# Weight sums by VectorE, later edge preparation, and a residual that is added from its two parts

## The reference

```python
xn = layernorm(x)                                            # 1250 x 1024
# graph part, 40000 edges (src, dst, type), 8 relations
u = xn @ root + bias
for r in range(8):                                           # mean of the neighbours of type r
    sums = segment_sum(xn[src] * (edge_type == r), dst)
    u = u + (sums / max(count_r, 1)) @ weight[r]
z = concat([u, xn]) @ w_gate + b_gate
gnn = tanh(u) * z + xn * (1 - z)
# linear attention, 16 heads of 64
q, k = elu(xn @ Wq) + 1, elu(xn @ Wk) + 1
v, g = xn @ Wv, sigmoid(xn @ Wg + bg)
mix = ((q * scale) @ (k^T v)) / clip(q . sum(k)) * g @ Wo
x1 = x + gnn + mix
# gated cell; the state starts at 0, so the forget gate falls out
y = layernorm(x1)
i, o, c = sigmoid(y @ Wi + bi), sigmoid(y @ Wo2 + bo), tanh(y @ Wc + bc)
out = x1 + o * tanh(i * c)
```

## Time and profile before

| what | us |
|---|---|
| median of the timed runs | 2199.6 |
| lowest and highest | 2197.4, 2200.03 |
| the profiled execution | 2188.48 |
| its span | 2186.7 |
| busy in it: TensorE, weight loads, VectorE, ScalarE, POOL | 2118.5, 1708.9, 1297.6, 538.6, 808.0 |

### The profile page before, as it was taken

How to read it: one execution, slowest core, us unless ns; L and a number is a source line. 1 busy time by engine, 2 the same in 40 slices (tenths; PEclk the granted TensorE clock), 3 DMA queues, 4 the chain that set the end, 5 groups by cost and what they waited for, 6 DMA issues and landing times.

```text
span 2186.7 us, 25371 instructions
## 1 busy us (share of the span) xinstructions
PE 2118.5 (97%) x9562; PEld 1708.9 (78%) x9562; DVE 1297.6 (59%) x1705; ACT 538.6 (25%) x749; POOL 808.0 (37%) x663
## 2 busy tenths in 40 slices
PE   7979897989999999999999999999999999999999
PEld 6767675768888888888877778888988887888887
DVE  5555778665666666666656666773354658534233
ACT  4433353501111111100121211012232313321121
POOL 3248134025555556543646445541211353000000
PEclk9999898999999999999999999999999999999999
DMA  7986675778588888883987878974159998604102
GB/s 273 344 282 196 220 248 173 250 206 303 173 288 309 314 295 308 280 288 116 317 281 270 279 260 296 306 229 163 61 172 263 282 294 270 175 23 126 56 34 80
DMA packets 248145, 497.68 MB, mean 228 GB/s; under 512 B 39442, under 2 KB 71873, under 8 KB 248023
## 3 DMA queue, kind: packets, MB, share of 16 engines
q1 hardware_dynamic: 165782, 279.20, 39.1%
q0 software_dynamic: 65248, 191.13, 26.2%
q10 hardware_dynamic: 16992, 25.73, 3.6%
HBM read 403.60 MB, written 133.45 MB: 246 GB/s over the span
## 4 chain that ended last, share of the span: by engine, by line
PE 90%; DVE 4%; DMA 2%; issue 1%; POOL 1%; SPq 1%; ACT 0%; POOLq 0%; ACTq 0%; DVEq 0%
PE acc L1412 71%; PE acc L1383 12%; PE acc L1407 5%; POOL runs L2375 1%; PE acc L1320 1%; DMA Wraw<-in_L_gnn_weight 1%; DVE Wlo L1708 1%; PE misc L1305 1%; DMA sample_d<-samples 1%; DMA made<-y_d 1%; SPq L861 0%; DVE below L1834 0%; PE tp L1267 0%; DMA runs<-code_d,run_row 0%; PE acc L1420 0%
## 5 line engine op out<-in xcount | busy, mean ns | idle before, releaser
L1412 PE MATMUL acc<-Whi,aThi 128*128 128x512 f32 (+1 forms) x2232 | 882.0, 395 | 0.0
L1412 PE MATMUL acc<-Whi,aTlo 128*128 128x512 f32 (+1 forms) x2232 | 879.1, 394 | 0.0
L1412 PE MATMUL acc<-Wlo,aThi 128*128 128x512 f32 (+1 forms) x2232 | 876.5, 393 | 0.0
L2395 POOL DMA_INDIRECT ring<-y_d,edge x390 | 484.1, 1241 | 425.7 <-DVE U L1984 144.1
L1412 PEld LDWEIGHTS acc<-Whi,aTlo 128*128 128x128 f32 (+1 forms) x2232 | 413.7, 185 | 103.5
L1412 PEld LDWEIGHTS acc<-Wlo,aThi 128*128 128x128 f32 (+1 forms) x2232 | 414.4, 186 | 102.4
L1412 PEld LDWEIGHTS acc<-Whi,aThi 128*128 128x128 f32 (+1 forms) x2232 | 413.6, 185 | 102.0 <-DVE made L1756 0.3
L1708 DVE TENSOR_TENSOR Wlo<-Wraw,Whi 128x1024 fp32r<-128x1024 f32 x176 | 224.0, 1275 | 161.1 <-ACT Whi L1438 160.2
L1383 PE MATMUL acc<-Whi,aThi 128*128 128x512 f32 (+2 forms) x560 | 229.4, 410 | 54.1 <-DVE Wlo L1708 33.1
L1984 DVE SCALAR_TENSOR_TENSOR U<-ring,edge,U 128x1024 f32<-128x1024 f32 x180 | 230.3, 1280 | 31.6 <-DMA ring<-y_d,edge 31.3
L1984 DVE SCALAR_TENSOR_TENSOR odd<-ring,edge,odd 128x1024 f32<-128x1024 f32 x170 | 217.7, 1280 | 36.4 <-DMA ring<-y_d,edge 35.9
(11 more groups left out here) (209 smaller groups left out, 1566.5 us busy)
## 6 DMA issues: line engine op xcount, KB each, us to landing
Wraw<-in_L_gnn_weight SPq DMA_DIRECT2D x80, 512.0 KB, 8.0
y_d<-res SPq DMA_DIRECT2D x80, 256.0 KB, 2.3
...
```

Of the source, the lines that this page charges most:

```text
L1412: mm = nc.tensor.matmul(to, a[:, k, rows(i)], b[:, s % 2, k, :], start=start, stop=stop)
L2395: pool.indirect_dma_start(ring[:, j % RING, :], None, a, bass.IndirectOffsetOnAxis(ap=index, axis=0), bounds_check=top - 1, oob_is_err=Fal ...
```

## The change

There are five parts.

1. The 32 weight sums are VectorE's, one per slot (q, k): for BE_ at units 3, 4 and 5 of the stage before, steps 1 and 5; for GA_0 at (39, 5) and (40, 5), for the others twenty units later each.
2. POOL no longer adds x + xnb, and xs_d is gone with its ten stores. The buffer of an x tile is free for the next load when the tile is normalised and turned.
3. In the output stage SP loads x into bias_sb and xn_d into the res buffer (`load_normal`, behind the wait that the store of unit q-3 has landed), and VectorE adds the two ahead of its wait for the product, then adds the product.
4. At the start SP issues five weight pieces before x1 instead of four, then three, then x2 and x3; the raw edges are loaded in unit 8.
5. The edge preparation is two units later, and tables_weights is cut into four pieces: (97, 7), (98, 2), (98, 6), (99, 2) and (126, 3), (126, 7), (127, 3), (127, 7).

```diff
-SUM_BESIDE = {BE_: (2, 2, 3, 3, 4, 5), GA_: (-1, 0)}
+SUM_BESIDE = {BE_: ((3, 1), (3, 5), (4, 1), (4, 5), (5, 1), (5, 5)), GA_: ((-1, 5), (0, 5))}
-READS_AT = 43
+READS_AT = 45
 def edge_at(q, k):
     if q < 36:
-        return divmod(212 + (8 * (q - 17) + k) * 21 // 16, 8)
-    return divmod(424 + (8 * (q - 36) + k) * 61 // 32, 8)
+        return divmod(228 + (8 * (q - 17) + k) * 21 // 16, 8)
+    return divmod(440 + (8 * (q - 36) + k) * 61 // 32, 8)
...
         # SP, at the start
         load_x(0)
-        for n in SPLIT_ORDER[0:4]:
+        for n in SPLIT_ORDER[0:5]:
             load_w(n)
         load_x(1)
-        load_w(SPLIT_ORDER[4])
-        load_w(SPLIT_ORDER[5])
+        for n in SPLIT_ORDER[5:8]:
+            load_w(n)
         load_x(2)
-        load_w(SPLIT_ORDER[6])
-        load_w(SPLIT_ORDER[7])
         load_x(3)
...
         def x_rows(t):
             sp.wait_ge(ln_done, with_halves(t))
             sp.dma_start(xn_d[side(t), :], xnb[0:SIDES[t % 5], t % XS, :]).then_inc(xn_st[t % XS], 16)
-            sp.wait_ge(xs_made, t + 1)
-            sp.dma_start(xs_d[side(t), :], xr[0:SIDES[t % 5], t % XS, :]).then_inc(xs_st[t % XS], 16)
         def next_x(t):
-            sp.wait_ge(xs_st[t % XS], 16 * (t // XS + 1))
+            sp.wait_ge(ln_done, with_halves(t))
             load_x(t + XS)
...
         # SP, output stage
-        sp.dma_start(bias_sb[0:width(t), t % 2, :], xs_d[rows(t), half(h)]).then_inc(xs_in[t % 2], 16)
+        sp.dma_start(bias_sb[0:width(t), t % 2, :], x[rows(t), half(h)]).then_inc(xs_in[t % 2], 16)
+        def load_normal(q):
+            s, t = UNIT[q]
+            free_res(sp, q)
+            sp.dma_start(res[0:width(t), q % 3, :], xn_d[rows(t), half(STAGE[s][2])]).then_inc(xs_in[t % 2], 16)
...
         # VectorE, evict(q)
+        if kind == O_:
+            dve.wait_ge(xs_in[i % 2], XS_FROM + 32 * (T // 2 * h + i // 2 + 1))
+            chain(nc.vector.tensor_tensor(bias_sb[0:w, i % 2, :], bias_sb[0:w, i % 2, :], res[0:w, q % 3, :],
+                                          ALU.add))
+            dve.wait_ge(prod, q + 1)
+            nc.vector.tensor_tensor(res[0:w, q % 3, :], p, bias_sb[0:w, i % 2, :], ALU.add).then_inc(evac_v, 1)
+            return
...
         # VectorE's list; add_quarters is POOL's of before, with nc.vector and dve
+        if (q, k) in SUMS_AT:
+            add_quarters(*SUMS_AT[q, k])
...
-        if (q, k) == edge_at(59 + 15 * h, 1):
-            tables_weights(h)
+        for piece in range(4):
+            if (q, k) == edge_at(58 + 15 * h, 4 + 2 * piece):
+                tables_weights(h, piece)
...
         # POOL
-        def rows_sum(t):
-            pool.wait_ge(ln_done, with_halves(t))
-            a = xr[0:SIDES[t % 5], t % XS, :]
-            nc.gpsimd.tensor_tensor(a, a, xnb[0:SIDES[t % 5], t % XS, :], ALU.add).then_inc(xs_made, 1)
```

More of the change, by code:

```diff
@@ L242 @@
 for _s in range(BLOCK_STAGES):
[L243 to L244 removed]
+    for (_g, _n), (_o, _k) in zip(SUM_ORDER.get(STAGE[_s][0], ()), SUM_BESIDE.get(STAGE[_s][0], ())):
+        SUMS_AT[FIRST[_s - 1] + _o, _k] = (_s, _g, _n)
 def sums_to(s, g, n):
@@ L434, in build @@
         x1n_d = dram("x1n_d", [N, D])
-        xs_d = dram("xs_d", [N, D])
         ax_d = dram("ax_d", [128, K, N])
@@ L601, in build @@
         xn_st = [sem(f"xn_st{i}") for i in range(XS)]
-        xs_st = [sem(f"xs_st{i}") for i in range(XS)]
-        ln_var, ln_root, ln_done, xs_made, x_turned, x_hi, x_lo = (
-            sem(n) for n in ("ln_var", "ln_root", "ln_done", "xs_made", "x_turned", "x_hi", "x_lo"))
+        ln_var, ln_root, ln_done, x_turned, x_hi, x_lo = (
+            sem(n) for n in ("ln_var", "ln_root", "ln_done", "x_turned", "x_hi", "x_lo"))
         t4_st = x1n_st = [sem(f"t4_st_x1n_st{i}") for i in range(2)]
@@ L1744, in lo_left, with add_quarters, add @@
                                         ALU.subtract).then_inc(a_lo, 1)
+            def add_quarters(s, g, n):
+                def add(to, of):
+                    nc.vector.tensor_tensor(to, to, of, ALU.add).then_inc(w_sum, 1)
+                kind, at = STAGE[s][0], GRAN * s + g
+                if kind == BE_ and n > 1:
+                    dve.wait_ge(w_sum, sums_to(s, g, n - 1))
+                    add(granule(Wraw, at) if n == 2 else granule(Whraw, at + 2), granule(Wraw, at + 2 if n == 2 else at))
+                    return
+                dve.wait_ge(w_raw[at % (2 * GRAN)], raw_to(at, 2))
+                if kind == BE_:
+                    dve.wait_ge(w_raw[(at + 2) % (2 * GRAN)], raw_to(at + 2, 2))
+                    add(granule(Wraw, at + 2), granule(Whraw, at))
+                else:
+                    add(granule(Wraw, at), granule(Whraw, at))
             def evict_middle(q):
@@ L2103, in evict @@
                 dve.wait_ge(prod, q + 1)
-                if kind == O_:
-                    n = T * h + i
-                    dve.wait_ge(xs_in[i % 2], XS_FROM + 16 * (T // 2 * h + i // 2 + 1))
-                    nc.vector.tensor_tensor(res[0:w, q % 3, :], p, bias_sb[0:w, i % 2, :], ALU.add).then_inc(evac_v, 1)
-                    return
                 n = BIASED.index(s)
@@ L2447, in _ @@
             pool.wait_ge(w_lo, 2 * GRAN)
-            rows_sum(0)
             for t in range(T):
@@ L2466, in _ @@
                            allow_small_or_imprecise_dtypes=True).then_inc(place_const, 1)
-            rows_sum(1)
-            for t in range(2, T):
-                rows_sum(t)
             for q in range(BLOCK_UNITS):
-                for s, g, n in SUMS_AT.get(q, ()):
-                    add_quarters(s, g, n)
                 reads = q - READS_AT
```

90 lines of the change are left out of this document (41 added, 49 removed).

## The result

The changed kernel takes 2174.43 us by the median of four timed runs (three lie between 2170.37 and 2174.65; the fourth took 4235.76, about twice as long, of unknown cause, and is left out of the ratio) against 2199.43 for four of before, a ratio of 0.988 (95% interval 0.986 to 0.990). The forecast was 2171, with a range from 2154 to 2188. Its profiled execution took 2174.2 us, with a span of 2172.4. The gain on the median is 25.0 us; between the two profiled executions it is only 14.3. Between the first two profiles the forecast's total hides two errors of 11 and 13 us that met; a second pair of profiles, further down, leaves less of both.

A forecast was written before the change was run, and what follows sets the result against it. TensorE was taken as the bound, busy 2118.5 of 2186.7 us, leaving at most 68.2 us idle to win. Terms summed to 28.0 us, giving 2160.5 profiled and, with 11.1 carried over, 2171; range 2154 to 2188.

The forecast's parts named there:

- start-up order: At the start, a weight piece before x1 shortens TensorE's 3.99 us stop: 1.9 us gained, between 0 and 2.5.
- rows_sum and xs_d, to unit 21: Without POOL's row sums and stores, tile 8 of x comes in time: 3.5 us gained, between 1 and 4.
- units 36 to 41: Block stage: Whraw lands earlier and six sums run faster on VectorE: 9.3 us gained, between 4 and 14.
- units 41 to 62: Block stage: uninterrupted reads and unstretched operations cut VectorE's wait for runs: 6 us gained, between 2 and 14.
- units 62 to 102: Block stage: tables(0) no longer stretched and tables_weights cut into pieces: 10.3 us gained, between 4 and 17.
- units 120 to 140, from unit 102: End of block stage: the second lump in pieces lets evictions in: 1 us gained, between -2 and +7.
- output stage: Last twenty units: added xn_d loads in a nearly full DMA, additions hidden on VectorE: -4 us, between 0 and -12.
- rival C: Output stage bound by its loads, landing 14.7 in every unit: 59.6 us lost, 2227 us; chance 0.06.
- The carried distance: Whole kernel: the timed median lies 11.1 us above the profiled execution, carried over from 2160.5 to 2171.6.
- A: Rival: nearly every stop goes, 46 us gained in all after 4 lost in the output stage, 2154 us; chance 0.18.
- D: Rival: nothing to measure; B's block stage, output stage losing 12, unit 60 worse by 4: 3 us, 2197; chance 0.07.
- B: Rival: VectorE's sums lengthen six reads by 13.6 us, units 60 and 100 stop nearly as before: 15 us, 2184; chance 0.19.

The follow-up runs named there:

- before_again: The kernel before, unchanged, run once more with a second profile; span 2195.2 us.
- after_again: The kernel after, unchanged, with a second profile; median 2170.13 us, ratio 0.989.
- after_start: The kernel after with weight pieces and x tiles loaded in the old order at the start, raw edges staying in unit 8; median 2175.49 us, ratio 0.992.
- after_xs: The kernel after with POOL's x plus xn sums, stored in xs_d, and raw edges loaded at the start again; median 2175.8 us, ratio 0.989.
- before_sums: The kernel before with only the weight sums moved to VectorE at the change's slots; median 2180.14 us, ratio 0.993.
- after_poolsums: The kernel after with the 32 weight sums on POOL again, at the units of before; median 2187.39 us, ratio 0.995.
- after_lump: The kernel after with tables_weights in one piece again, at (99, 0) and (127, 5); median 2170.82 us, ratio 0.988.
- after_8rows: The kernel after with each output-stage load of xn_d fetching 8 rows instead of up to 128; median 2158.33 us, ratio 0.982.
- after_early: The kernel after with the edge preparation two units earlier, as in before, tables_weights still in four pieces; median 2176.03 us, ratio 0.990.

## Why the prediction was right, and where it was not
By its own steps, in us gained between the two first profiles (before to after) and between the two second ones (before_again to after_again), as differences of unit starts:

| step | predicted | first pair | second pair | shown by |
|---|---|---|---|---|
| start-up order | 1.9 | 3.8 | 4.4 | after_start: 1.7 to 3.4 of it at unit 3 |
| rows_sum and xs_d, to unit 21 | 3.5 | 4.3 | 6.0 | after_xs: 9.8 lost again by unit 21 |
| units 36 to 41 | 9.3 | 4.7 | 9.7 | before_sums, after_xs |
| units 41 to 62 | 6 | 9.5 | 6.2 | after_poolsums: 10.7 of the sums |
| units 62 to 102 | 10.3 | 11.1 | 11.5 | after_poolsums: 3.9 of the sums |
| units 120 to 140, from unit 102 | 1 | -2.0 | -0.2 | after_lump: nothing |
| output stage | -4 | -17.2 | -8.9 | after_8rows: 12 to 16 of what the loads move |
| sum | 28.0 | 14.3 | 28.7 | |

So single terms move by up to 5 us, and the output stage by 8, from one pair of executions to the other; errors of a term below that can't be told from scatter.

**The block stage** was forecast at 32.0 and gave 31.5 in the first pair, with four of its terms off by 1.9 to 4.6 us in both directions, and 37.6 in the second, with the terms of units 36 to 102 within 1.2 us. Its mechanisms held: VectorE's operations of 2.47 are 0.37 again, the reads are not interrupted, tile 8 comes in time. Of its signs these came too: the waits for splits under 20 us (10.9), the wait for runs under 12 (6.19), the reads within 30 us of their first (29.4), a stop left at unit 130 (2.56 and 2.64). Two statements were wrong. VectorE did not stand in front of the first sum for 8 us or more: it came there at 127.34, held up by its wait of 8.19 us for ax_d at 108.66 and the conversions behind it, and found the load in. And the gain of units 62 to 102 was credited to the stretched tables and to the cut lump; the sums on POOL account for 3.9 of it, and the lump, by unit 141, for none. In after_poolsums only one of the six operations was stretched (2.46), since the tables two units later miss most of the sums, and after_early loses 4.7 in that stretch. By my reading the later places do there what was credited to the other edit, and since the two edits cover the same stretch, their prices don't add; no run has both undone.

**The output stage** is the step that failed. The term was -4, and the stage lost 17.2 in the first pair, 8.9 in the second, 13.3 by the means of seven kernels against seven. In the first profile after, TensorE stopped there four times for 13.2 us, over the 10 that the prediction had named as a sign of being wrong and more than the one stop it allowed; in the second it had four waits too, two of them above 1 us, for 7.8 in all. "With the median landing of 6.9 it takes 10.3" took the landing of single loads and a loop that fits by 0.8 us, in a stage whose DMA share was 0.93 and 1.00 before anything was added. The median landing hardly moved (5.7 for x and 6.8 for xn_d now), but the longest was 18.8, for a load of xn_d, and VectorE waited 20.4 us for such loads. The prediction had a better number in hand, 19 to 21 us of DMA time for 5.12 MB in 115 us: of it 8 to 17 was lost. The range of the term, 0 to -12, holds the second pair and not the first; rival C named the mechanism, with its price too high, since it let every load land last.

**The carried distance** is the other error. The 11.1 us between before's profiled execution and its median were taken to hold for both kernels. before_again and after show that they were before's scatter. Without the carry the forecast would have been 2160.5; with it and the first pair's 17.2 in place of 4 it would have been 2185. That the total came within 3.4 us of 2174.43 is partly luck: in the first pair a base that was too short by 11 us met an output stage priced too low by 13; in the second pair a block stage that gave 5.6 us more than forecast met an output stage 4.9 too low.

**Rivals.** A (nearly every stop goes) did not come: the block stage gained 31.5 and 37.6 us of A's 50. D did not come either, since it needs B's block stage. B (reads lengthened by VectorE's sums) is refuted in its size and not in its mechanism: in after two reads were lengthened by sums, 0.5 us in all, against the 13.6 that B took. B also put six reads against operations as long as the 2.76 of a large split, and its 2.27 a read is 3.57 less 1.30, where 1.00 is the time of a read without its issue. Over the profiles of this study a read of runs that begins inside a VectorE operation with two SBUF inputs, and is lengthened, ends 0.86 to 0.92 us after it (the first read of an execution 1.14 to 1.16); of two that began 0.05 and 0.06 us after such an operation one was not lengthened (1.00, before_again) and one was (3.57, before). The warning of the Trainium skill ("SBUF — State Buffer", section "SBUF: two separate sides") that GpSimd can't write descriptors while VectorE holds the shared ports would lengthen any read that a sum falls beside, and the trace does not agree (0.99 for the read at 183.50 with a sum from 183.63). Its narrower wording, that these inputs exclude only a GpSimd operation that reads SBUF, is what the trace agrees with, if a read counts as one through its row numbers in run_row (1.39 for a read begun inside a sum; and two splits took 4.45 beside a row sum of POOL in before_sums and 2.36 without one in after).

**Open.** The size of the sums alone on the kernel before (ratio 0.993, but unit 141 only 1 to 6 us earlier); 4 to 7 of the 10.9 us between after_xs and before_sums at unit 141 that neither the start order (2 to 4) nor the places of the edge steps (2 to 3) explain; and what lengthens the two stores into ax_d in these two kernels.
